# A two-block attention and expert kernel: fp32r maxima, queries prepared inside the attention loop, routing on un-normalised rows, running counts, one delay per group and step

## The chip, the cores and the metric

One core of one Trainium2 chip. The time is device microseconds (us) of one execution, as the median of several runs; fewer is better. The engines are TensorE (PE, with its weight loads as PEld), VectorE (DVE), ScalarE (ACT), GpSimd (POOL) and SyncE (SP), each with an instruction queue of its own that is worked off in order, and the DMA queues.

## The reference

`x` is (2, 512, 128) and `ctx_1024` is (2, 77, 128), fp32. Two blocks run one after the other; each adds an attention and then a layer of experts to `x`:

```
x = x + xattn0(layernorm(x), ctx)        # 16 heads of 8, rotary, a bias, layernorm again inside, gate
x = x + ffn0(layernorm(x))               # top 2 of 8 experts, 128 -> 512 -> 128, silu
x = x + xattn1(layernorm(x), ctx, ctx)   # 16 heads of 8, biases, no gate
x = x + ffn1(layernorm(x))               # top 2 of 8, capacity 321 rows an expert
```

Inside `xattn0` the output is `gate * attended + (1 - gate) * residual` with `gate = sigmoid(attended @ Wgate.T + b_gate)`, where `residual` is the normalised input. The softmax is over 77 keys. The router takes the normalised rows times a (128, 8) matrix, picks two experts by value, and weights their outputs by a softmax over the two.

## The kernel before

The 1,024 tokens are 8 tiles of 128, in 4 **groups** (g = 0 to 3) of 256 tokens. Each block has an attention loop of 16 **units** u (4 per group: four heads at a time), then a tail in which the last groups are finished, then the experts.

**A turn of the loop.** On TensorE (`attention` in the tensor block), turn u does, in this order: `shifted_scores(u)` (L1166, 4 matmuls of 256 columns, in block 0 each with two more of 128 for the bias), `maxima(u+1)` (L1158: the row maxima found by VectorE are turned by two fp32 matmuls of 128 columns against the identity), `scores(u+2)` (L1142), `attend(u-2)` (L1188, 16 small matmuls), and then the steps that are due. VectorE's `attention(u)` (L800) takes the maximum over the scores; ScalarE's (L640) copies the turned maxima into the stack `qst` (L638) and takes the exponential (L654). `scores(u)` waits for the maximum of u-1, `shifted_scores(u)` for the exponential of u-1 and the copied maxima of u.

**The steps.** When a group's four units are attended, ScalarE copies numerator and denominator (L649), and then: `attended` (DVE: reciprocal L813, product L814), `project` (PE), in block 0 `projected` (ACT, then DVE), `gate` (PE) and `tanh` (ACT), then `residual` (DVE: new rows, their statistics), `deviation` (POOL: the reciprocal deviation, L500/L501), `hidden` (DVE: normalised rows, L796/L850), `copies` (ACT), `turn` (PE: transposes of the rows), `turned` (ACT), `logits` (PE), `choose` (DVE: top two), `ranks` (PE: a count of all earlier picks, 1 to 8 matmuls a tile), `slots` (DVE) and `send` (POOL: four indirect DMAs a group). Tables at L71 to L80 give each step on each engine a delay in turns after the group's last unit, one number for all groups, in some cases another for group 3. `due` (L111) goes through the names in the table's order and yields those that fall due. In each engine's queue everything else waits behind a step that waits.

**Queries.** Before a block's loop, the rows are transposed (`tokens`), projected (`queries`), in block 0 rotated (DVE, with the sum on POOL, L566), split into a high and a low part and stacked (`stack`, 8 matmuls of 256 columns, L1310) for groups 0 and 1; groups 2 and 3 follow in the first turns (L83 to L101). In block 0 the rows are normalised twice, with statistics taken of the once normalised rows (L1054 to L1066).

**Warm-ups.** `warm_up` (L1130) are matmuls on zeros: 13 at the start, 12 before block 1, 2 in each turn of block 1's tail, 3 before the experts. They are there for TensorE's clock.

After the tail come the experts (`rows_in`, `up`, `down`), the results go back by indirect DMA, are gathered, and VectorE combines them; block 1 begins with that.

Of the kernel before, what the change touches and what calls it, by code (L numbers as in the profile page):

```python
# [6 lines left out]
B, T, D = 2, 512, 128  # L7
KV = 77
# [35 lines left out]
WARM_START = 13  # L44
WARM_SUM = 12
WARM_TAIL = [0, 2]
# [24 lines left out]
PE_STEPS = [dict(gate3=5, project=4, gate=7, turn=9, logits=10, ranks=11, next_context=8, next_parts=10,  # L71
                 next_keys=11, turn3=7, logits3=9, ranks3=10),
            dict(project=4, turn=7, logits=7, ranks=9)]
DVE_STEPS = [dict(attended=5, projected3=6, residual3=7, hidden3=9, projected=8, residual=9, hidden=10,
                  choose=12, slots=13, next_context=11, next_parts=13, next_keys=14, choose3=11, slots3=12),
             dict(attended=5, residual=7, hidden=8, choose=10, slots=11)]
ACT_STEPS = [dict(projected3=4, tanh3=5, projected=5, tanh=7, copies=8, turned=9),
             dict(copies=9, turned=7)]
POOL_STEPS = [dict(deviation=10, residual=12, send=15),
              dict(deviation=5, residual=7, send=10)]  # L80


PE_QUERIES = [[(-1, "tokens", 0), (-1, "queries", 0), (-1, "keys", 0), (-1, "tokens", 1), (-1, "tokens", 2),  # L83
               (-1, "queries", 1), (-1, "stack", 0), (-1, "queries", 2), (-1, "tokens", 3), (-1, "stack", 1),
               (0, "queries", 3), (1, "stack", 2), (2, "stack", 3)],
              [(-1, "tokens", 0), (-1, "queries", 0), (-1, "tokens", 1), (-1, "tokens", 2), (-1, "queries", 1),
               (-1, "stack", 0), (-1, "tokens", 3), (-1, "queries", 2), (-1, "stack", 1), (0, "queries", 3),
               (1, "stack", 2), (2, "stack", 3)]]
ACT_QUERIES = [[(-1, "tokens", 0), (-1, "keys", 0), (-1, "tokens", 1), (-1, "high", 0), (-1, "tokens", 2),
                (-1, "high", 1), (-1, "stack", 0), (-1, "tokens", 3), (-1, "high", 2), (-1, "stack", 1),  # L90
                (0, "high", 3), (1, "stack", 2), (2, "stack", 3)],
               [(-1, "tokens", 0), (-1, "keys", 0), (-1, "high", 0), (-1, "tokens", 1), (-1, "high", 1),
                (-1, "tokens", 2), (-1, "stack", 0), (-1, "tokens", 3), (-1, "high", 2), (-1, "stack", 1),
                (0, "high", 3), (1, "stack", 2), (2, "stack", 3)]]
DVE_QUERIES = [[(-1, "rotated", 0), (-1, "keys", 0), (-1, "rotated", 1), (-1, "stack", 0), (-1, "rotated", 2),
                (-1, "bias", 0), (-1, "stack", 1), (0, "rotated", 3), (1, "stack", 2), (1, "stack", 3),
                (3, "keys", 1)],
               [(-1, "sum", 0), (-1, "sum", 1), (-1, "norm", 0), (-1, "sum", 2), (-1, "norm", 1),
                (-1, "sum", 3), (-1, "norm", 2), (-1, "norm", 3), (-1, "low", 0), (-1, "low", 1),
                (-1, "stack", 0), (-1, "low", 2), (-1, "stack", 1), (0, "low", 3), (1, "stack", 2),  # L100
                (2, "stack", 3)]]  # L101

WEIGHT_TURNS = [[6, 7, 8, 9], [3, 4, 5, 6]]


def at_turn(queries, turn):

    return [(name, g) for when, name, g in queries if when == turn]


def due(steps, u):  # L111

    for name, delay in steps.items():
        g, rest = divmod(u - delay - (UG - 1), UG)
        if name[-1] == "3":
# [1391 lines left out]
```

## Time and profile before

| | us |
|---|---|
| median of 3 runs | 326.11 |
| lowest and highest of them | 325.69, 334.38 |
| span of the profiled execution | 324.3 |
| TensorE busy | 250.7 |
| VectorE busy | 155.1 |
| GpSimd busy | 137.8 |
| ScalarE busy | 118.2 |

The span is from the first to the last instruction of one profiled execution, and the median includes what lies around it. Busy times overlap between engines.

### The profile page before, as it was taken

How to read it: one execution, taken by the hardware profiler on the slowest of the kernel's cores; microseconds unless marked ns; L12 is line 12 of the kernel's file. 1: busy time of each engine (PE TensorE's matmuls, PEld its weight loads, DVE VectorE, ACT ScalarE, POOL GpSimd, SP SyncE). 2: the span in 40 equal slices, each digit the busy share in tenths (PEclk: the TensorE clock that was granted, in tenths of full speed). 3: DMA queues.
4: the chain of work that ended last, by engine and by line, in shares of the span. 5: the costliest groups of instructions: out<-in, count | busy, mean ns of one | idle time of the engine just before them, and what ended most of it. 6: DMA issues, size and time to landing. Idle time of an engine off the chain costs nothing.

```text
span 324.3 us, 5466 instructions
## 1 busy us (share of the span) xinstructions
PE 250.7 (77%) x2044; PEld 197.2 (61%) x2044; DVE 155.1 (48%) x497; ACT 118.2 (36%) x206; POOL 137.8 (42%) x178
## 2 busy tenths in 40 slices
PE   2767999999975539999942989989987338999800
PEld 2645766667754427999941775545555328999800
DVE  3878425363775364242211964276878303332205
ACT  4033637755321023443500067965540204423200
POOL 5744602630156441355562400641267631456640
PEclk9999999999975558999995799999999959999975
DMA  7999970200011017000013920200010125001015
GB/s 241 269 224 377 219 161 2 65 3 2 0 36 34 33 33 197 16 20 26 23 36 127 361 116 0 66 1 2 0 37 33 33 82 141 15 31 36 26 29 181
DMA packets 26819, 27.02 MB, mean 83 GB/s; under 512 B 3193, under 2 KB 23844, under 8 KB 26534
## 3 DMA queue, kind: packets, MB, share of 16 engines
q1 hardware_dynamic: 23797, 21.58, 24.6%
q0 software_dynamic: 2560, 4.08, 3.9%
q10 hardware_dynamic: 432, 0.98, 0.9%
q8 instruction: 18, 0.29, 0.4%
q14 instruction: 12, 0.09, 0.1%
HBM read 16.76 MB, written 10.79 MB: 85 GB/s over the span
## 4 chain that ended last, share of the span: by engine, by line
PE 49%; issue 20%; DVE 13%; DMA 6%; POOL 5%; ACT 3%; another core or an unknown queue 1%; SPq 1%; POOLq 0%; DVEq 0%; ACTq 0%
PE ps L1201 8%; PE ps L1406 6%; PE ps L1178 6%; PE ps L1395 5%; PE ps L1162 4%; PE ps L1153 4%; PE ps L1133 3%; PE ps L1184 2%; DMA xres<-x 2%; DMA xe<-back 2%; DVE cst L813 2%; DMA sent<-hidk,slotu 1%; DVE attT L814 1%; PE ps L1217 1%
## 5 line engine op out<-in xcount | busy, mean ns | idle before, releaser
L559 POOL DMA_INDIRECT back<-probT,pairu x48 | 46.5, 970 | 37.4 <-DVE probT L992 15.1
L1133 PE MATMUL ps<-blank,ident 128*128 128x256 f32 x90 | 28.6, 479 | 23.6 <-DMA sent<-hidk,slotu 13.0
L1406 PE MATMUL ps<-w,hT 128*128 128x128 f32 (+1 forms) x384 | 45.0, 274 | 0.0
L804 DVE TENSOR_REDUCE peak<-ps 128x8 f32<-128x616 f32 x32 | 25.5, 798 | 40.2 <-PE ps L1153 40.2
L1406 PEld LDWEIGHTS ps<-w,hT 128*128 128x128 f32 (+1 forms) x384 | 44.2, 183 | 0.0
L654 ACT ACTIVATE probT<-ps 77x1024 f32<-77x1024 f32 x32 | 32.7, 1022 | 27.7 <-PE ps L1184 15.5
L518 POOL DMA_INDIRECT sent<-hidk,slotu x32 | 31.9, 997 | 16.4 <-issue 9.8
L1133 PEld LDWEIGHTS ps<-blank,ident 128*128 128x128 f32 x90 | 21.1, 244 | 28.5 <-issue 14.0
L531 POOL TENSOR_TENSOR w1lo<-hT,w1hi 128x1024 fp32r<-128x1024 f32 x8 | 18.9, 2366 | 40.0 <-ACT w1hi L628 40.0
L1178 PE MATMUL ps<-qst,kst 100*78 100x256 f32 x128 | 29.1, 300 | 1.0 <-ACT qst L638 1.0
L500 POOL TENSOR_SCALAR vare<-mv 128x2 f32<-128x2 f32 (+2 forms) x17 | 3.8, 226 | 52.8 <-DVE mv L786 52.3
L696 ACT ACTIVATE hT<-ps,col 128x384 f32<-128x384 f32 x32 | 17.3, 582 | 24.1 <-PE ps L1395 24.1
L696 ACT ACTIVATE hT<-ps 128x321 f32<-128x321 f32 x32 | 13.3, 441 | 33.2 <-PE ps L1395 33.0
L1395 PE MATMUL ps<-xhi,w1hi 128*128 128x384 f32 (+1 forms) x64 | 22.2, 346 | 1.5 <-DVE xlo L981 1.5
L1178 PEld LDWEIGHTS ps<-qst,kst 100*78 100x78 f32 x128 | 16.9, 148 | 8.4 <-issue 5.8
L1162 PE MATMUL ps<-ident,peak 128*4 128x128 f32 x128 | 19.2, 273 | 2.9 <-DVE peak L804 2.9
L1201 PE MATMUL ps<-probT,vpad 77*32 77x256 f32 x256 | 21.0, 391 | 0.0
L1395 PE MATMUL ps<-xhi,w1lo 128*128 128x384 f32 (+1 forms) x64 | 20.8, 325 | 0.0
L1395 PE MATMUL ps<-xlo,w1hi 128*128 128x384 f32 (+1 forms) x64 | 20.8, 325 | 0.0
L1201 PE MATMUL ps<-probT,onepad 77*32 77x256 f32 x256 | 20.2, 379 | 0.0
L992 DVE TENSOR_TENSOR probT<-ps,row 128x128 f32<-128x128 f32 x24 | 5.5, 285 | 26.6 <-PE ps L1406 23.2
L995 DVE COPY probT<-ps 128x128 f32<-128x128 f32 (+1 forms) x24 | 5.5, 284 | 25.4 <-PE ps L1406 21.9
(158 smaller groups left out, 474.1 us busy)
## 6 DMA issues: line engine op xcount, KB each, us to landing
sent<-blank SPq DMA_DIRECT2D x16, 193.5 KB, 8.5
xe<-sent SPq DMA_DIRECT2D x16, 193.5 KB, 4.0
back<-blank SPq DMA_DIRECT2D x16, 128.0 KB, 4.8
hT<-w1b SPq DMA_DIRECT2D x4, 512.0 KB, 6.0
w<-w2b SPq DMA_DIRECT2D x1, 2048.0 KB, 13.5
xe<-back SPq DMA_DIRECT2D x8, 256.0 KB, 3.5
hT<-w1d SPq DMA_DIRECT2D x4, 512.0 KB, 5.5
w<-w2d SPq DMA_DIRECT2D x1, 2048.0 KB, 11.4
```

Of the source, the lines that this page charges most:

```text
L518: pool.indirect_dma_start(sent[m], bass.IndirectOffsetOnAxis(ap=slotu[:, t, k:k + 1], axis=0), hidk[:, t, k, :], None, bounds_check=NSLOT ...
L531: pool.tensor_tensor(w1lo[:, w, :], raw[:, k % RAWS], w1hi[:, w, :].bitcast(F32), ALU.subtract)\
L559: pool.indirect_dma_start(back[m], bass.IndirectOffsetOnAxis(ap=pairu[0:n, e, c:c + 1], axis=0), ye[0:n, e, c, :], None, bounds_check=NPAI ...
L654: act.activation(probT[0:KV, u % RING].rearrange("p (i q) t -> p i (q t)", i=2), ps[0:KV, BK:BK + 2, :], ACT.Exp).then_inc(s_exp[a], 1)
L696: act.activation(hT[:, e % 2, f, 0:CAP[m]], ps[:, 2 + n % 4, 0:CAP[m]], ACT.Silu, bias=bias).then_inc(s_silu[m], 1)
L804: dve.tensor_reduce(peak[:, u % 2], s, AX.X, ALU.max, negate=True).then_inc(s_peak[a], 1)
L1133: pe.matmul(ps[:, bank, 0:GQ], ident[:], blank[:, 0:2, 0:D], start=True, stop=True)
L1162: last = pe.matmul(ps[ST:ST + Q4, BK + u % 2, i * P:(i + 1) * P], peak[:, u % 2, i, :], ident[:], start=True, stop=True)
L1178: last = pe.matmul(ps[0:KP, BK + q // 2, GQ * (q % 2):GQ * (q % 2) + GQ], kst[0:ST + Q4, b, Q4 * j + q, :], qst[0:ST + Q4, j, at:at + GQ], ...
L1201: last = pe.matmul(ps[32 * q:32 * q + 32, bank, 0:GQ], w, probT[0:KV, u % RING, q, :], start=(j == 0), stop=(j == UG - 1))
L1395: last = pe.matmul(ps[:, 2 + n % 4, 0:EVEN[m]], w[:, e, f * P:(f + 1) * P], x[:, e % 2, 0:EVEN[m]], start=(i == 0), stop=(i == len(parts) ...
L1406: last = pe.matmul(ps[0:n, 6 + e % 2, c * P:(c + 1) * P], hT[:, e % 2, f, c * P:c * P + n], w2[:, e, f, :], start=(f == 0), stop=(f == FC ...
```

## The change

- **Maxima** are turned by fp32r matmuls (`peak` and the identity are fp32r), into a PSUM bank of their own.
- **PSUM**: numerator and denominator share one bank (`BND`); `stack` always uses banks 6 and 7; the routing of groups 2 and 3 uses banks 5 and 1.
- **Queries**: only group 0 is made before the loop (and group 1's tokens in block 0); the rest is spread over turns 0 to 9. In block 0 the two normalisations become one (`twice_normed`, from one set of statistics), the rotary sum and the low part go from POOL to DVE, the bias parts from DVE to POOL, the once normalised rows are made in turns 1 and 4. In block 1 the sums of groups 2 and 3 fall in turns 0 and 3. The exponential's table is loaded ahead of the waits.
- **Router**: `turn` transposes the new rows themselves, not the normalised ones; both routers are multiplied by a centring matrix once, in block 0's turn 8, and `choose` scales the logits by the row's reciprocal deviation.
- **Ranks**: a running count of earlier picks; 2 to 3 matmuls a tile.
- **Delays** are given for each group and step; `due` goes through the groups first, then the names. Sends of a group may fall in two halves.
- **Warm-ups**: 6 at the start, 5 and 3 before block 1, a few in the queries' preparation, none behind the loops.

The core of the diff:

```diff
-WARM_START = 13
-WARM_SUM = 12
-WARM_TAIL = [0, 2]
+WARM_START = 6
+WARM_BACK = 3
+WARM_QUERIES = [dict(tokens=1, queries=0, keys=0, stack=3, scores=2), dict(tokens=0, queries=1, stack=2, scores=1)]
+WARM_SUM = 5
...
-PE_STEPS = [dict(gate3=5, project=4, gate=7, turn=9, logits=10, ranks=11, next_context=8, next_parts=10,
-                 next_keys=11, turn3=7, logits3=9, ranks3=10),
-            dict(project=4, turn=7, logits=7, ranks=9)]
-DVE_STEPS = [dict(attended=5, projected3=6, residual3=7, hidden3=9, projected=8, residual=9, hidden=10,
-                  choose=12, slots=13, next_context=11, next_parts=13, next_keys=14, choose3=11, slots3=12),
-             dict(attended=5, residual=7, hidden=8, choose=10, slots=11)]
-ACT_STEPS = [dict(projected3=4, tanh3=5, projected=5, tanh=7, copies=8, turned=9),
-             dict(copies=9, turned=7)]
-POOL_STEPS = [dict(deviation=10, residual=12, send=15),
-              dict(deviation=5, residual=7, send=10)]
+PE_STEPS = [dict(project=(4, 4, 3.5, 4), gate=(6, 6, 4, 6), turn=(8, 8, 6, 7), logits=(9, 9, 7, 7), ranks=(11, 10, 9, 8),
+                 next_context=(0, 0, 0, 9), next_parts=(0, 0, 0, 10), next_keys=(0, 0, 0, 11)),
+            dict(project=(4, 4, 3.5, 4), turn=(7, 6, 4, 5), logits=(8, 7, 5, 5), ranks=(10, 8, 6, 6))]
+DVE_STEPS = [dict(attended=(5, 5, 5, 5), projected=(7, 7, 6, 7), residual=(9, 9, 7, 9), choose=(12, 11, 10, 10),
+                  hidden=(12, 11, 12, 10), slots=(14, 12, 12, 11),
+                  next_context=(0, 0, 0, 12), next_parts=(0, 0, 0, 13), next_keys=(0, 0, 0, 14)),
+             dict(attended=(5, 5, 5, 5), residual=(7, 7, 6, 7), choose=(11, 10, 7, 8), hidden=(11, 10, 10, 8),
+                  slots=(13, 11, 10, 9))]
+ACT_STEPS = [dict(projected=(5, 5, 4, 4), tanh=(7, 7, 5, 6), turned=(9, 9, 7, 7), copies=(11, 10, 11, 8)),
+             dict(turned=(8, 7, 5, 5), copies=(10, 9, 8, 6))]
+POOL_STEPS = [dict(deviation=(9, 9, 7, 10), send=(14, 12, 13, 12), send_second=(14, 12, 15, 12)),
+              dict(deviation=(7, 7, 6, 10), send=(13, 11, 13, 12), send_second=(13, 11, 15, 12),
+                   residual=(14, 14, 17, 13))]
...
+PE_QUERIES = [[(-1, "tokens", 0), (-1, "queries", 0), (-1, "tokens", 1), (-1, "keys", 0), (-1, "stack", 0),
+               (0, "queries", 1), (1, "tokens", 2), (3, "stack", 1), (4, "queries", 2), (4, "tokens", 3),
+               (6, "stack", 2), (7, "queries", 3), (9, "stack", 3)],
+              [(-1, "tokens", 0), (-1, "queries", 0), (-1, "stack", 0), (0, "tokens", 1), (1, "queries", 1),
+               (3, "stack", 1), (4, "tokens", 2), (5, "queries", 2), (6, "stack", 2), (7, "tokens", 3),
+               (8, "queries", 3), (9, "stack", 3)]]
...
+DVE_QUERIES = [[(-1, "rotated", 0), (-1, "values", 0), (-1, "low", 0), (-1, "keys", 0), (-1, "stack", 0),
+                (0, "norm", 1), (0, "rotated", 1), (1, "hidden", 0), (2, "low", 1), (3, "stack", 1),
+                (4, "rotated", 2), (4, "hidden", 1), (5, "low", 2), (5, "keys", 1), (6, "stack", 2),
+                (7, "rotated", 3), (8, "low", 3), (9, "stack", 3)],
+               [(-1, "sum", 0), (-1, "sum", 1), (-1, "norm", 0), (-1, "norm", 1), (-1, "low", 0), (-1, "stack", 0),
+                (0, "sum", 2), (1, "norm", 2), (2, "low", 1), (3, "stack", 1), (3, "sum", 3), (4, "norm", 3),
+                (5, "low", 2), (6, "stack", 2), (8, "low", 3), (9, "stack", 3)]]
+
+CENTRE_TURN = 8
+WEIGHT_TURNS = [[5, 6, 7, 9], [3, 4, 5, 7]]
...
-    for name, delay in steps.items():
-        g, rest = divmod(u - delay - (UG - 1), UG)
...
+    for g in range(GROUPS):
+        for name, delays in steps.items():
+            if delays[g] and u == UG * g + UG - 1 + delays[g]:
+                yield name, g
...
-        peak = sb("peak", [P, 2, GT, Q4])
+        peak = sb("peak", [P, 2, GT, Q4], F32R)
...
+                dve.wait_ge(s_rstd, group[0] + 1)
+                for t in range(GT * g, GT * g + GT):
+                    lp = ps[:, route_bank(g), t % GT * E:t % GT * E + E]
+                    if m == 0:
+                        last = dve.scalar_tensor_tensor(out=logit[:, t, :], in0=lp, scalar=rstd[:, t:t + 1], in1=gbias[:],
+                                                        op0=ALU.mult, op1=ALU.add)
...
             for u in range(turns(DVE_STEPS[0])):
                 attention(0, u)
+                if u == CENTRE_TURN + AHEAD:
...
-                    last = pe.matmul(ps[ST:ST + Q4, BK + u % 2, i * P:(i + 1) * P], peak[:, u % 2, i, :], ident[:],
-                                     start=True, stop=True)
+                    at = GQ * (u % 2) + i * P
+                    last = pe.matmul(ps[0:Q4, BMX, at:at + P], peak[:, u % 2, i, :], identr[:], start=True, stop=True)
...
             def turn(m, g):
-                pe.wait_ge(s_hid[m], g + 1)
...
+                pe.wait_ge(s_xnew[m], g + 1)
+                if m == 0 and g == 0:
+                    pe.wait_ge(s_rout, 2)
+                if g == 1:
+                    pe.wait_ge(s_slot[m], 1)
...
+                transposed(route_bank(g), lambda k: xres[:, GT * g + k, :], GT).then_inc(s_hTp[m], 1)
...
+                earlier = [(ones, before[:, g, :])] if g >= 1 else []
                 for k in range(GT):
...
+                    last = summed(P + k * E, earlier + [(ones, picked[:, t + i, :]) for i in range(k)]
+                                  + [(tri, picked[:, t + k, :])])
...
                     query_steps(a, u + 2)
+                    steps_due(u - 0.5)
                     if u + 1 < UNITS:
                         maxima(a, u + 1)
```

## Rows read from the trace of the kernel before

**Rows 1.** Windows by stage: from:to, length, busy us of each engine, PEclk, DMA.
```profile
0.00:32.20 32.20, 19.34 (x116) 15.21 (x116) 22.40 (x87) 9.64 (x16) 17.10 (x41) 1.00 1.04 278
32.20:90.70 58.50, 57.85 (x590) 39.57 (x590) 28.57 (x58) 32.50 (x49) 18.11 (x15) 1.00 0.31 64
90.70:120.70 30.00, 16.02 (x116) 12.35 (x112) 17.27 (x83) 5.66 (x12) 16.68 (x19) 0.56 0.11 36
...
194.00:242.50 48.50, 45.58 (x452) 26.21 (x450) 30.48 (x76) 30.29 (x44) 17.09 (x16) 1.00 0.06 18
242.50:264.50 22.00, 9.96 (x74) 7.50 (x70) 10.26 (x50) 3.64 (x8) 15.11 (x17) 0.85 0.10 33
```

**Rows 2.** Timeline, a turn of block 0: start, length, engine, line, operation.
```profile
44.74 0.29 PE L1184 MATMUL ps<-btok,bkey 98*78 98x128 f32 x2
44.87 0.29 PE L1178 MATMUL ps<-qst,kst 100*78 100x256 f32 x1
...
45.75 0.60 PE L1162 MATMUL ps<-ident,peak 128*4 128x128 f32 x4
...
46.28 0.55 PE L1153 MATMUL ps<-kst,qst 96*128 96x312 f32 x2
...
47.95 0.29 PE L1184 MATMUL ps<-btok,bkey 98*78 98x128 f32 x2
```

**Rows 3.** Groups of instructions by line: count, busy us, mean ns, idle before.
```profile
L804 DVE TENSOR_REDUCE peak<-ps 128x8 f32<-128x616 f32 x32 | 25.5, 798 | 40.2 <-PE ps L1153 40.2
...
L813 DVE RECIPROCAL cst<-cst 128x256 f32<-128x256 f32 x8 | 14.0, 1744 | 0.0
```

**Rows 4.** Source line 414 (the last router load) and block 0's first shifted scores.
```profile
L414 SPq DMA_DIRECT2D router<-wr x1: 490/490/490, 4.6 to 4.6; - x1
...
DMA to landing us min/median/max: 8.4/8.4/8.4
...
32.21 0.34 PE L1178 MATMUL ps<-qst,kst 100*78 100x256 f32 x1 [0.34 <-ACT qst L638]
```

**Rows 5.** Timeline, late in block 0, and the last send in the chain.
```profile
73.72 0.36 PE L1178 MATMUL ps<-qst,kst 100*78 100x256 f32 x1
...
84.21 0.43 DVE L814 TENSOR_TENSOR attT<-cst 128x256 f32<-128x256 f32 x1
...
85.17 0.39 ACT L661 ACTIVATE norm<-ps 128x256 f32<-128x256 f32 x1 [1.65 <-PE ps L1227]
...
94.51 0.42 DVE L814 TENSOR_TENSOR attT<-cst 128x256 f32<-128x256 f32 x1
...
118.10 2.45 DMA sent<-hidk,slotu
```

**Rows 6.** Block 1: timeline, and the chain's wait behind the last ranks.
```profile
176.73 8.42 PE L1133 MATMUL ps<-blank,ident 128*128 128x256 f32 x24 [10.63 <-DMA xe<-back]
...
194.05 0.63 PE L1178 MATMUL ps<-qst,kst 100*78 100x256 f32 x4
...
216.24 0.72 PE L1178 MATMUL ps<-qst,kst 100*78 100x256 f32 x4
...
245.55 0.42 DVE L814 TENSOR_TENSOR attT<-cst 128x256 f32<-128x256 f32 x1
...
254.56 2.23 another core or an unknown queue
...
262.31 2.24 DMA sent<-hidk,slotu
```

**Rows 7.** Windows of 2 and 1 us around two idle times of TensorE.
```profile
28.00:30.00 2.00, 0.15 (x2) 0.13 (x3) 1.90 (x5) 0.42 (x2) 0.64 (x1) 1.00 1.10 461
...
94.00:95.00 1.00, 0.01 (x1) 0.01 (x1) 0.96 (x3) 0.00 (x0) 0.38 (x1) 0.52 0.08 29
```

**Rows 8.** Source line 814: shortest, median and longest product of eight, in ns; POOL's low weights.
```profile
L814 DVE TENSOR_TENSOR attT<-cst x8: 424/425/2041, 55.8 to 245.5; 128x256 f32<-128x256 f32 x8
...
L531 POOL TENSOR_TENSOR w1lo<-hT,w1hi 128x1024 fp32r<-128x1024 f32 x8 | 18.9, 2366 | 40.0 <-ACT w1hi L628 40.0
```

## What was predicted before the run

> **What bounds the kernel now.** I read the windows by stage first, then the timeline of each stage, then the chain. Each block has a preparation, an attention loop, a tail, and experts with their sends. In both loops TensorE is busy nearly all the time (57.85 of 58.5 us, 45.58 of 48.5) and VectorE half or more of it; in the tails TensorE is busy half the time, and in block 0's, which has no warm-ups, at a clock of 0.56 against 0.85 in block 1's [rows 1]. A turn of block 0 takes 3.21 us (47.95 less 44.74). The maxima hold TensorE for 0.53 of them (45.75 to 46.28); the scores and attending take what is left to the next turn, 1.5 [rows 2]. On VectorE a turn needs one maximum, 0.80 [rows 3], so it has some 2 us a turn for steps. In the tails the order is a single file: attended, project, residual, turn, logits, choose, ranks, slots, sends. The experts and what lies behind them aren't touched. I count in four marks for each block: the first shifted scores, those of a later turn (12 in block 0, 8 in block 1), the last `attT`, and the landing of the last send.
>
> **Fp32r maxima.** The nearest row for the new form is the pair of bias matmuls, also fp32r with 128 columns: the next matmul starts 0.13 after the pair (44.74 to 44.87) [rows 2]. So 0.53 becomes 0.13, less 0.40 a turn, if TensorE is what the turn waits for: 12 turns to the second mark give 4.8 in block 0, 8 give 3.2 in block 1. Bounds: 0, where another engine sets the turn, and 0.40 in all 32 turns, 12.8.
>
> **Block 0, preparation.** The rows of one normalisation are ready at about 10.8 instead of 15.7 (one set of statistics and one pass less). But TensorE also waits for all row loads before the loop, and the last, issued at 4.6, lands 8.4 later, at 13.0 [rows 4]; that is late next, and the gain is cut by 2.2. From 13.0 I follow the queues with the lengths that these steps have in the trace: tokens and their copy 1.5, queries 1.1, rotation and sum on VectorE 1.3, `values` 0.9 (it lies ahead of `low`), low part, krep and stack_keys to 19.7, the stacks to 20.5, scores at 20.6, their maximum till 22.0. Behind it VectorE makes batch 1's rows (1.1), and TensorE has `tokens 2`, which waits for them, ahead of the first shifted scores: 23.6 against 32.2 [rows 4]. **-8.6**. Bounds: -6 (POOL's bias parts, which now stand between, late, or the clock half for a time) and -11 (no wait for batch 1).
>
> **Block 0, turns 0 to 11.** Before: 32.21 to 73.72, 41.5 [rows 4, 5]. Taken off: 4.8. Added to TensorE inside the loop: three stacks, two projections and one set of tokens, 5.3, less the stack that was there, 1.0; group 0's `turn` and the centring, 0.7. The first four turns wait for VectorE, which has a maximum and 1.1 to 2.4 of other work in each (rows of batch 1, two rotations, `hid`, `keys`), and `stack 3` and `project` of group 1 wait too: its `attended` now stands behind `residual` of group 0 on VectorE, since `due` goes by groups. Together 2.3. Sum -4.8 + 5.0 + 2.3: **+2.5** (bounds 0 and +5).
>
> **Block 0, turn 12 to the last `attT`.** Before: 73.72 to 94.93, 21.2. Here the order costs. In the trace the product of group 2 is done at 84.6, before group 1's tanh even starts (85.17) [rows 5]. Now both `residual` of group 1 (4+3+9) and `attended` of group 2 (8+3+5) fall in turn 16 of VectorE, and the residual comes first. It waits for the tanh, which on ScalarE stands behind the exponential of turn 14, the maxima of 15 and now `copies` of group 0 (0.4). In time from turn 12's start: tanh done 11.4, residual and statistics 13.1, reciprocal 1.74 [rows 3] and product 15.4. TensorE has `project` of group 2 at 14.5, ahead of three attends, ready from 11.9: a wait of 3.5. Queued behind it: attend 13, turn, gate of group 2 (1.5, which now also precedes attend 14), attend 14, logits, attend 15, done at 21.8 instead of 16.9. ScalarE's numerator copy waits for nothing worse, but VectorE has choose (1.5), hidden (0.6), residual (1.7) and slots (0.9) ahead of the last `attended`: 27.8. **+6.6**. Bounds: 0 (the tanh gets through early) and +9.
>
> **Block 0, tail.** Before: 94.93 to 120.55, 25.6 [rows 5]. Now groups 1 and 2 are further on. After `attT`: project and yT 2.3, gate 2.9 at the low clock, tanh and new rows 1.4, turn, copy and logits 2.2, choose 1.6, ranks 0.5, slots 0.9, sends 5.4, landing 2.45, with the waits between them 20.2. Gone from the path are statistics, deviation and normalised rows ahead of `turn` (some 2.3), group 2's choose ahead of group 3's, and most of the count: the last ranks and the wait behind them stand for some 2.2 to 2.6 (the chain's wait of 2.23 in block 1 [rows 6]). **-5.4** (bounds -2 and -9). Block 0 together -4.9.
>
> **Block 1.** *Preparation*: TensorE is in warm-ups until 185.15 (176.73 and 8.42 [rows 6]) while the first rows are ready at 181.2. With 5 for 12 they are over by then, 3.7 to the good. `norm 1` no longer waits for group 2's sum, only one stack precedes the scores, and the table load (1.3) lies ahead of the rows: first shifted scores at 188.3 for 194.05: **-5.8** (bounds -3.5 and -8). *Turns 0 to 7*: before 22.2 (194.05 to 216.24 [rows 6]). -3.2 for the maxima, +3.7 for the queries' work inside, +3.0 of waits: `sum` (2.0) ahead of maxima 1 and 4 on VectorE, `tokens 2` and `stack 2` behind them. **+3.5**. *Turn 8 to the last `attT`*: before 29.7. -3.2; group 1's `turn` in turn 13 waits for `slots` of group 0, which VectorE has in turn 16, behind choose, hidden, residual and a maximum, 3.0; group 2's turn, logits and choose are now ahead of the last reciprocal, 1.7. **+1.5**. *Tail*: before 18.6 (245.97 to 264.55). No statistics ahead of `turn`, fewer counts, against a deviation that on POOL stands behind two of group 2's sends (2.5), and transposes and logits at the lower clock (0.44 and 0.61 in this tail, 0.66 and 1.02 in block 0's): **-1.9**. Block 1 together -2.7.
>
> **What lies beside.** The running count (two small additions) and the router's scaling (0.2 each) are behind work that no one waits for; the shared bank `BND` holds as many matmuls as the two before. The keys for block 1 now follow the last slots on VectorE; they end some 2 us before the first expert rows are there. That cover gone, each further us is one.
>
> **The sum.** -4.9 - 2.7 = -7.6 on the span of 324.3: 316.7. The median lies 1.8 above that span: 318.5.
>
> **Two rules.** The trace shows the clock at 0.52 in the window 94.0 to 95.0, in which TensorE was busy for 0.01, but at 1.00 in 28.0 to 30.0, busy for 0.15 [rows 7]. The Trainium skill, "TensorE: Matmul & The Clock Gate", section "What's actually happening", says that the throttled state is the default and that activity lifts it; by that rule the waits of 3.5 and 3.0 above, and the tail without warm-ups, all fall to the low clock, and the rows agree only in part. What it would do here is the third rival.
> The trace has the product of `attended` at 0.42 mostly and once at 2.04, where POOL's low weights (2.37) ran [rows 8]. The Trainium skill, "SBUF — State Buffer", section "SBUF: two separate sides", says that VectorE's operations with two SBUF inputs and GpSimd's share a port pair that one holds for its whole instruction. The rotary sum and the low part become such operations on VectorE, beside POOL's bias parts; by that rule they lose up to one POOL instruction each, the trace agrees for the product, and the range has it.
>
> **Rivals.** *(a) The forecast*, 312 to 325: 0.48.
> *(b) The waits aren't met*: VectorE keeps up, the product of group 2 and the slots of block 1 come in time. Then the +6.6 is -1.6, the +2.3 and the +3.0 (twice) go: about -24 in all, 302; half of it 310. For it speaks that VectorE is busy in only half of the loop [rows 1]; against it, that these waits come from the order in the queues, not from load. 300 to 312: 0.25.
> *(c) Nothing measurable*: the gains in the preparation are given back whole in the loops, by waits at their upper bounds (+5, +9) and by locks. 323 to 332: 0.17.
> *(d) Slower: the clock.* In each wait inside the loops TensorE falls to its low level. A turn then costs 2.8 more than its 2.8. Three turns in all at the low level eat the gain of 7.6; from a little over five (14.5 by 2.8) it is slower by 2%: 333. Against it speaks that the clock stayed at 1.00 through the idle 28.0 to 30.0 [rows 7] and through both loops [rows 1]. 0.10.
>
> **Range and chances.** (a), (b) without its best part, and the near part of (c) give 303 to 328. A change under about 2% (6.5 us) can't be told from none here, so faster means under 319.6: all of (b) and two thirds of (a), 0.57; within 2%: a third of (a) and most of (c), 0.32; slower: (d) and the end of (c), 0.11.
>
> **What would show it.** Maxima: the next matmul 0.13 behind them, and a plain turn of 2.8 in block 0, 2.3 in block 1. Preparation: first shifted scores near 23.6, and 5.8 nearer to the gathered rows in block 1. Order: TensorE idle before group 2's project in block 0 and before group 1's turn in block 1, 3 us each. Clock: 1.00 in both loops. The forecast is wrong if those idle times are missing (then b), if the clock line dips inside a loop (then d), or if a plain turn keeps its 3.2.

## The result, and the profile after

| | before | changed |
|---|---|---|
| median of 4 runs, us | 326.2 | 339.98 |
| lowest and highest | 325.69, 334.38 | 336.5, 347.23 |
| span of the profiled execution | 324.3 | 335.3 |

The ratio is 1.033, 95% interval 1.030 to 1.036: slower by 3.3%, where 318.5 was forecast. (The ratio compares the undisturbed executions, of the changed kernel those of 336.5 and 337.05, and so do all ratios below; `e5_stall` and `e11_lock` have no ratio on record, and their two undisturbed times are given.)

Windows of the changed kernel by the stages of [rows 1]: length, busy us of PE, PEld, DVE, ACT, POOL, the granted clock, DMA.

```profile
0.00:23.80 23.80, 15.39 (x86) 11.99 (x87) 14.98 (x53) 6.90 (x10) 12.94 (x38) 1.00 1.03 250
23.80:88.00 64.20, 54.93 (x536) 40.76 (x536) 39.81 (x82) 33.42 (x52) 18.14 (x13) 0.92 0.40 105
88.00:125.40 37.40, 24.58 (x143) 15.63 (x141) 16.85 (x91) 4.97 (x12) 18.02 (x20) 0.50 0.09 29
...
197.00:244.00 47.00, 41.01 (x348) 27.30 (x349) 27.09 (x67) 27.31 (x42) 13.01 (x11) 0.79 0.04 12
244.00:275.50 31.50, 15.73 (x110) 8.90 (x108) 15.37 (x80) 6.91 (x13) 19.86 (x24) 0.50 0.10 33
```

Both loops of the kernel before had TensorE at 1.00 and, in block 0, busy for 57.85 of 58.5 [rows 1]. Now the first loop is at 0.92 with 9 us idle, the second at 0.79, and the last attends have slipped into the stretches at 0.50. Windows of 3 us tell where the clock falls:

```profile
48.00:51.00 3.00, 0.60 (x3) 0.60 (x4) 3.00 (x2) 0.94 (x1) 2.07 (x1) 0.86 0.45 149
51.00:54.00 3.00, 3.00 (x19) 2.19 (x22) 2.13 (x3) 1.30 (x2) 0.00 (x0) 0.50 0.02 5
54.00:57.00 3.00, 3.00 (x19) 1.96 (x12) 0.70 (x2) 0.58 (x2) 2.35 (x1) 0.50 0.00 0
57.00:60.00 3.00, 2.97 (x36) 2.13 (x36) 0.94 (x3) 1.56 (x3) 0.00 (x0) 1.00 0.00 0
84.00:87.00 3.00, 0.07 (x1) 0.07 (x1) 2.89 (x7) 0.71 (x1) 0.94 (x2) 0.55 0.00 0
87.00:90.00 3.00, 3.00 (x18) 2.13 (x22) 1.03 (x6) 0.47 (x1) 1.25 (x1) 0.50 0.01 3
...
194.00:197.00 3.00, 1.66 (x11) 0.91 (x9) 2.51 (x8) 1.91 (x4) 0.93 (x2) 0.99 0.03 14
197.00:200.00 3.00, 2.37 (x11) 2.29 (x12) 0.57 (x2) 1.06 (x2) 0.00 (x0) 0.50 0.00 0
209.00:212.00 3.00, 3.00 (x22) 2.19 (x14) 0.52 (x2) 1.24 (x3) 2.36 (x1) 0.50 0.00 0
```

In each place TensorE idles first (0.60 busy of 3, 0.07 of 3, 1.66 of 3), and what follows is done at 0.50, although TensorE is busy for 3.00 of 3 again (2.37 in the window 197 to 200). In the window 51 to 54 it gets through 19 matmul records, in 57 to 60 through 36. The timeline of the changed kernel names the waits (in brackets: idle time and what ended it):

```profile
44.22 2.38 POOL L557 TENSOR_TENSOR w1lo<-hT,w1hi 128x1024 fp32r<-128x1024 f32 x1 [4.07 <-ACT w1hi L665]
44.48 2.41 DVE L1029 TENSOR_TENSOR q<-q,ropeb 128x256 f32<-128x256 f32 x1
47.73 2.34 POOL L557 TENSOR_TENSOR w1lo<-hT,w1hi 128x1024 fp32r<-128x1024 f32 x1 [1.12 <-ACT w1hi L665]
47.99 2.36 DVE L1038 TENSOR_TENSOR qlo<-q,qhi 128x256 fp32r<-128x256 f32 x1 [0.39 <-ACT qhi L760]
50.40 0.53 PE L1409 MATMUL ps<-qhi,sel 128*96 128x256 f32 x1 [2.52 <-DVE qlo L1038]
...
83.09 0.43 DVE L878 SCALAR_TENSOR_TENSOR hidb<-norm,hidb 128x256 f32<-128x256 f32 x1 [2.94 <-ACT norm L701]
83.55 0.42 DVE L880 SCALAR_TENSOR_TENSOR xres<-hidb,base 128x256 f32<-128x256 f32 x1
...
84.70 1.72 DVE L858 RECIPROCAL hid<-hid 128x256 f32<-128x256 f32 x1
86.45 0.42 DVE L859 TENSOR_TENSOR attT<-hid 128x256 f32<-128x256 f32 x1
86.93 1.22 PE L1291 MATMUL ps<-attT,sqw 128*128 128x256 f32 x2 [3.27 <-DVE attT L859]
...
242.60 0.66 PE L1215 MATMUL ps<-identr,xres 128*128 128x128 f32 x2 [2.90 <-DVE slotu L950]
```

There are three kinds. (1) VectorE's rotary sum and low part of group 3 begin 0.26 behind GpSimd's subtraction and end 0.28 behind its end. They take 2.41 and 2.36, where the rotary sum takes 0.43 and the low part 0.41 to 0.92 in the other groups: the last stack is 2.5 late. (2) The order: group 1's residual and statistics ahead of group 2's reciprocal, so `project` of group 2 waits 3.27 (the prediction's 3.5), and group 1's `turn` in block 1 waits 2.90 for group 0's slots (the prediction's 3.0). (3) In block 1's first turns there are four short waits in a row, 0.67, 1.14, 0.72 and 0.62. Behind each kind, TensorE's work takes about twice as long.

In turns without extra steps or waits the change does what it says. The maxima are followed at 0.12 (22.58 to 22.70), and units 3 to 4 are 2.77 apart, against 3.20 in [rows 2].

### The profile page after: what moved, and what is told of

It is laid out like the page before. It is cut to its first block, busy times and chain, and to the rows that moved or that the text cites. A ratio compares the mean times of both kernels' runs of the same rounds, so it can differ in the third digit from the quotient of the medians.

```text
span 335.3 us, 5249 instructions
## 1 busy us (share of the span) xinstructions
PE 250.8 (75%) x1911; PEld 197.2 (59%) x1911; DVE 159.4 (48%) x506; ACT 117.1 (35%) x206; POOL 134.7 (40%) x175
## 4 chain that ended last, share of the span: by engine, by line
PE 53%; DVE 16%; issue 12%; POOL 8%; DMA 5%; ACT 4%; POOLq 1%; DVEq 0%; SPq 0%; ACTq 0%
PE ps L1514 9%; PE ps L1275 8%; PE ps L1503 8%; PE ps L1256 5%; PE ps L1210 4%; POOL back L584 4%; PE ps L1409 3%; PE ps L1232 2%; POOL sent L544 2%; PE ps L1262 2%; DMA xe<-back 2%; DMA back<-probT,pairu 2%; PE ps L1215 2%; DVE hid L858 2%; PE ps L1304 1%
## 5 line engine op out<-in xcount | busy, mean ns | idle before, releaser
L849 DVE TENSOR_REDUCE peak<-ps 128x8 fp32r<-128x616 f32 x32 | 25.4, 793 | 37.0 <-PE ps L1232 37.0
L1210 PE MATMUL ps<-blank,identr 128*128 128x256 f32 x60 | 22.3, 529 | 17.8 <-DMA sent<-hidk,slotu 9.1
L1256 PE MATMUL ps<-qst,kst 100*78 100x256 f32 x128 | 31.6, 324 | 1.0 <-ACT qst L675 0.5
L526 POOL TENSOR_SCALAR vare<-mv 128x2 f32<-128x2 f32 (+1 forms) x13 | 2.9, 226 | 65.7 <-DVE mv L831 65.7
L1210 PEld LDWEIGHTS ps<-blank,identr 128*128 128x128 f32 x60 | 15.1, 269 | 21.9 <-issue 9.9
L1275 PE MATMUL ps<-probT,vpad 77*32 77x256 f32 x256 | 25.1, 470 | 0.0
L1256 PEld LDWEIGHTS ps<-qst,kst 100*78 100x78 f32 x128 | 18.7, 163 | 9.6 <-ACT qst L675 6.3
L1275 PE MATMUL ps<-probT,onepad 77*32 77x256 f32 x256 | 24.3, 459 | 0.0
L1232 PE MATMUL ps<-kst,qst 96*128 96x312 f32 x64 | 17.7, 360 | 0.5 <-ACT qst L768 0.4
## 6 DMA issues: line engine op xcount, KB each, us to landing
w<-w2d SPq DMA_DIRECT2D x1, 2048.0 KB, 11.1
```

What stands on the lines that cost most here:

```text
L849: dve.tensor_reduce(peak[:, u % 2], s, AX.X, ALU.max, negate=True).then_inc(s_peak[a], 1)
L1210: pe.matmul(ps[:, bank, 0:tiles * D], ident, blank[:, 0:tiles, 0:D], start=True, stop=True)
L1232: last = pe.matmul(ps[:, BS + i, 0:Q4 * KP], qst[0:ST, j, at + i * P:at + (i + 1) * P], kst[0:ST, b, Q4 * j:Q4 * j + Q4, :].rearrange("p q ...
L1256: last = pe.matmul(ps[0:KP, BK + q // 2, GQ * (q % 2):GQ * (q % 2) + GQ], kst[0:ST + Q4, b, Q4 * j + q, :], qst[0:ST + Q4, j, at:at + GQ], ...
L1275: last = pe.matmul(ps[32 * q:32 * q + 32, BND, den * GQ:den * GQ + GQ], w, probT[0:KV, u % RING, q, :], start=(j == 0 and not den), stop=( ...
```

## Experiments

Each run is compared with the kernel before on the same chip; in brackets the 95% interval.

**Fillers in front of the waits** (`e1_fill`).

```diff
+FILL_QUERIES = [{('stack', 3): 4}, {'maxima 0': 1, 'maxima 1': 2, ('stack', 1): 1, ('tokens', 2): 1}]
+FILL_STEPS = [{('project', 2): 6}, {('turn', 1): 5}]
+            def fill(n, half):
+                for _ in range(n):
+                    pe.matmul(ps[64:P, BMX, GQ * half:GQ * half + GQ], ident[:, 64:P], blank[:, 0:2, 0:D],
+                              start=True, stop=True)
```

> The changed kernel with short matmuls on zeros put in front of seven of TensorE's waits inside the two loops (4 before the last stack and 6 before group 2's project in block 0; 1, 2, 1 and 1 in the first turns and 5 before group 1's turn in block 1), about as long as the idle times there. No wait is shortened and no work is taken away. Theory A (the clock): the idle times bring TensorE to its low level, and the turns behind them run at 0.50 of the clock. Then both loops stay at 1.00, the stretches 50.4 to 57.1, 86.9 to 99.2, 197 to 214.7 and 242.6 to 256.4 shrink by about 3, 5, 6 and 5, and the kernel takes 318 to 325, less than the kernel before. Theory B (only the waits and the work that was moved): the clock is a by-product, the kernel takes 335 to 342 as the changed one, or more by what the fillers add.

Measured: 325.52, ratio 0.997 (0.990 to 1.004): 3.6% or 12 us less than the changed kernel, by adding work only, and at the upper end of what theory A gave. Windows with the filled waits in it:

```profile
48.00:51.00 3.00, 2.60 (x17) 1.60 (x15) 2.63 (x2) 1.79 (x3) 2.35 (x1) 1.00 0.62 175
84.00:87.00 3.00, 2.46 (x19) 1.57 (x21) 2.25 (x8) 0.24 (x1) 0.55 (x1) 1.00 0.00 0
197.00:200.00 3.00, 3.00 (x32) 2.05 (x31) 2.44 (x9) 1.49 (x4) 0.93 (x2) 1.00 0.03 5
239.00:242.00 3.00, 1.51 (x23) 0.73 (x23) 2.82 (x12) 0.78 (x2) 0.88 (x3) 0.97 0.07 22
```

From 33 on the clock stays up until the last attends (before that, 27 to 30 is at 0.50, see the last section), and what TensorE waits for isn't there sooner (the product of group 2 ends at 85.5, 15.0 behind unit 12, and in the changed kernel too it is 15.0). Theory A holds and gives the size: the low clock behind the waits costs 12 us (13.9 in the loops of the two traces), all of the 11 that the changed kernel lost. Without it the change is worth nothing measurable.

**A wait in the kernel before** (`e5_stall`), with nothing of the change:

```diff
+AGAIN = [{8: 6}, {6: 2}]
+                    for n in range(AGAIN[a].get(u, 0)):
+                        n = 6 * a + n
+                        dve.tensor_reduce(wover[:, n, :].rearrange("p (i q) -> p i q", i=GT), s, AX.X, ALU.max, negate=True)
```

> The kernel before, with nothing of the change: VectorE repeats the maximum of unit 8 of block 0 six more times (into a tile that nothing reads) and that of unit 6 of block 1 twice more. VectorE has about 1.3 to spare in a turn, so TensorE should wait some 3.3 once in block 0 and under 1 once in block 1. Theory A (clock): behind the wait in block 0 TensorE runs at 0.50 for several us; the kernel takes the 4 of the waits and at least 3 more, 333 or more. Theory B (only waits): 330 to 331, with the clock at 1.00 in both loops. If the short wait in block 1 alone brings the clock down too, the length of a wait isn't what decides.

Measured: 334.53 and 335.13, the second with the trace, span 333.4 (the kernel before had 325.9 on that chip); the median of all four executions is 345.6.

```profile
58.03 0.49 PE L1166 MATMUL ps<-ident,peak 128*4 128x128 f32 x3 [2.94 <-DVE peak L808]
```

```profile
54.00:57.00 3.00, 1.09 (x12) 0.95 (x11) 3.00 (x5) 1.43 (x2) 2.35 (x1) 1.00 0.02 5
57.00:60.00 3.00, 1.97 (x14) 0.99 (x18) 2.97 (x4) 1.31 (x2) 0.00 (x0) 0.80 0.60 168
60.00:63.00 3.00, 3.00 (x19) 1.93 (x12) 0.80 (x2) 0.10 (x1) 2.35 (x1) 0.50 0.02 7
63.00:66.00 3.00, 3.00 (x18) 2.41 (x17) 0.00 (x0) 0.93 (x1) 0.00 (x0) 0.57 0.00 0
```

One wait of 2.94 brings the clock down, and the kernel takes some 9 us more (theory A: 333 or more). Units 7 to 12 take 25.5 instead of 19.6: 2.9 of wait and 3.0 behind it. The last send of block 0 is 4.8 late. Another 4, not shown to come from the wait, lie in the two experts' stretches, which took 58.6 and 61.6 here and 56.2 and 59.8 in the trace of before. The short wait in block 1 was 0.67 and left the clock at 1.00.

**GpSimd's subtraction moved** (`e3_weights`), `-WEIGHT_TURNS = [[5, 6, 7, 9]` to `+WEIGHT_TURNS = [[4, 8, 9, 10]`.

> The changed kernel with the casts of the expert weights of block 0 in turns 4, 8, 9 and 10 instead of 5, 6, 7 and 9, so that GpSimd's subtraction of 1024 columns (2.37) doesn't run while VectorE has the rotary sum and the low part of group 3. Theory of the port: both VectorE operations go from 2.4 to about 0.42, the wait of 2.5 before the last stack goes. With theory A (clock) the stretch at 0.50 from 51 to 57 goes too: shifted scores of unit 12 start 6 to 8 sooner than 71.9. With theory B they start 2.5 to 4 sooner. Rival: the VectorE operations are slow for another reason (their operands), and stay at 2.4.

Measured: 340.44, ratio 1.042 (1.037 to 1.048). The rotary sum went to 0.43 in all four groups, the wait before the last stack is gone, and unit 8 started at 52.35 instead of 57.12. But the last subtraction now met the residual, whose first operation waits for the tanh at the same time:

```profile
63.08 2.36 POOL L557 TENSOR_TENSOR w1lo<-hT,w1hi 128x1024 fp32r<-128x1024 f32 x1 [1.78 <-ACT w1hi L665]
63.31 2.41 DVE L878 SCALAR_TENSOR_TENSOR hidb<-norm,hidb 128x256 f32<-128x256 f32 x1 [1.53 <-ACT norm L701]
```

```profile
66.00:69.00 3.00, 0.44 (x2) 0.20 (x2) 2.90 (x8) 0.00 (x0) 0.96 (x2) 0.79 0.00 0
69.00:72.00 3.00, 2.87 (x13) 2.69 (x14) 0.79 (x2) 0.00 (x0) 0.00 (x0) 0.50 0.00 0
...
87.00:90.00 3.00, 3.00 (x29) 1.96 (x18) 1.49 (x6) 1.33 (x4) 0.00 (x0) 0.50 0.00 0
```

The wait came back 16 us later, as 1.53 and 2.46 up to 66.2 and 69.1, and the clock stayed at 0.50 from there to the end of the loop. The theory of the shared port holds for a third operation, which again ends 0.28 behind the subtraction; the rival, that the operations are slow by their operands, is out. An operation with one input in PSUM keeps its length beside the same subtraction (which ran from 56.17 to 58.53):

```profile
56.55 0.42 DVE L868 TENSOR_TENSOR hidb<-ps,hidb 128x256 f32<-128x256 f32 x1 [1.54 <-issue]
```

The gain was lost to the same two effects. That unit 12 would start 6 to 8 sooner was a miss: it started at 70.9, 1 sooner.

**`attended` first** (`e2_order`), in `due`:

```diff
+    return sorted(found, key=lambda step: step[0] != "attended")
```

> The changed kernel, where of the steps due in one turn an `attended` comes first (so group 2's reciprocal and product no longer stand behind group 1's residual on VectorE in turn 16 of block 0). Theory A (clock): the wait of 3.3 before group 2's project goes, and with it the low clock behind it: the last attT of block 0 lands 7 to 9 nearer, at 95 to 97 instead of 104.2, and the kernel is 6 to 9 us faster than the changed one, some 330. Theory B (waits only): it is 3 faster, 335 to 337, with the clock still low from 84 on. If the wait only moves to the next step, nothing changes.

Measured: 340.46, ratio 1.020 (1.010 to 1.030). The traced execution took 346.7, so only the order and the waits are read from it; the two that the ratio goes by took 330.95 and 335.08. The wait before group 2's project is gone and from unit 15's shifted scores to the last `attT` it is 14.0 instead of 21.8. In block 1 the same rule puts slots behind a reciprocal, and the wait before group 1's `turn` grows from 2.90 to 5.05. The ratio is 1.3% or some 4 us better than the changed kernel's, between B's 3 and A's 6 to 9, and the intervals touch. In the trace the clock was low from 51 on already. So this run doesn't tell A from B.

**fp32 maxima again**, in the changed kernel (`e4_fp32`) and with the fillers (`e8_fill_fp32`): `peak` as plain fp32, `ident` for `identr`.

> The changed kernel with the maxima turned by fp32 matmuls again, everything else of the change kept. If the turn is TensorE's: 0.40 more in each of some 25 turns that wait for nothing, 8 to 10 us slower than the changed kernel. If other engines or the waits set the turns: 0 to 4 slower. Theory A adds that more TensorE work in a turn could hold the clock up; then it could even be even with the changed kernel.

> The kernel with the fillers inside the loops, with the maxima turned by fp32 matmuls as before the change. With the clock held, the price of this form can be read alone. If TensorE sets the turns: 0.40 more in each of some 25 turns, 333 to 336. If other engines set them: 326 to 329.

Measured: 1.039 (1.031 to 1.047) against the changed kernel's 1.033, no difference that these runs resolve. With the fillers 1.023 (1.014 to 1.032) against 0.997: 2.6%, 8.4 us. Its stages are longer by 3.2 and 0.6 in block 0's loop and 2.4 and 2.0 in block 1's, 8.2 in all, and units 3 to 4 are 3.20 apart again. The saving of 0.40 a plain turn was real; in the changed kernel it doesn't show. Why fp32 cost so little there (more TensorE work between the waits, or shorter waits) isn't settled. The mean granted clock of the executions of `e4_fp32` that the ratio goes by, 0.83 to 0.85 for the changed kernel's 0.81, points to the first.

**Fillers in the tails** (`e7_tail`): `+WARM_BEFORE = [dict(project=7, gate=4, turn=5, ranks=12), dict(project=12, turn=6, ranks=12)]`. And the kernel before without its own (`e10_no_tail`): `WARM_TAIL = [0, 0]`.

> The kernel with the fillers inside the loops, and with matmuls on zeros also before four or three of group 3's steps in the tails (7, 4, 5 and 12 matmuls of 128 columns in block 0, 12, 6 and 12 in block 1). Theory A for the tail: the clock of 0.50 is what the tails' TensorE steps pay (project, gate, turn and logits of group 3 take 2.1, 2.9, 0.7 and 1.0 there, and half of that at 1.00), so each tail is 2 to 3 shorter: 320 to 322. Rival: the zeros keep TensorE busy at its low level when the step is due, and each tail is 0 to 3 longer: 325 to 331.

> The kernel before with the one edit that takes the warm-ups from block 1's tail. If they held the clock for steps on the path (project, turn and logits of the last group): 1 to 2.5 slower. If the tail is set by VectorE, ScalarE, GpSimd and the sends: no difference, within 1.

Measured: `e7_tail` 0.998 (0.994 to 1.003), no gain on 0.997. The clock was up in it, at 1.00 from 102 to 111 where the run without had 0.50, and still the tails took 21.4 and 15.9 as without. In block 0 the rival is what the traces show: TensorE's `project` and `gate` are on the path there, the gate took 1.7 instead of 2.9, but `project` started 1.25 behind its product instead of 0.06, because zeros were still being worked off at 0.50 before it. The gate ended 6.1 behind the product instead of 6.2. In block 1 TensorE is off the path: group 3's deviation waits on GpSimd for two sends of group 2 in both runs, and starts 5.0 and 5.2 behind the product. What the tails would take at full clock with no zeros in the way was not measured. `e10_no_tail` 1.006 (1.002 to 1.011), 2 us; its traced tail is 17.9 against 18.6, so the 2 us aren't found there, and the traced execution, 324.4, was the fastest of its ten.

**Waits taken away instead of filled** (`e6_all`, `e9_steps`, `e12_no_fill`, `e11_lock`). `e9_steps`, cut to its core (parts of the table lines, with comments added):

```diff
-WEIGHT_TURNS = [[5, 6, 7, 9]
+WEIGHT_TURNS = [[4, 8, 9, 11]
+    return sorted(found, key=lambda step: step[0] != "attended")
-turn=(7, 6, 4, 5), logits=(8, 7, 5, 5)            # TensorE, block 1
+turn=(7, 7, 4, 5), logits=(8, 8, 5, 5)
-residual=(7, 7, 6, 7), hidden=(11, 10, 10, 8), slots=(13, 11, 10, 9)   # VectorE, block 1
+residual=(7, 8, 6, 7), hidden=(13, 10, 10, 8), slots=(12, 11, 10, 9)
-hidden=(12, 11, 12, 10)                           # VectorE, block 0
+hidden=(12, 13, 12, 10)
+FILL_QUERIES = [{}, {'maxima 0': 1, 'maxima 1': 2, ('stack', 1): 1, ('tokens', 2): 1}]
+FILL_STEPS = [{('turn', 2): 1}, {}]
```

`e6_all` has the same casts, `attended` first in block 0 alone, the first of the other moves, much the same fillers in the loops, and the tails' fillers; `e12_no_fill` is `e9_steps` without a filler; `e11_lock` is `e9_steps` with the casts in turns 5, 6, 7 and 9.

> The changed kernel with its waits taken away where the traces show them, rather than filled: casts of the expert weights in turns 4, 8, 9 and 11 (no GpSimd subtraction beside a VectorE operation with two SBUF inputs), `attended` first in block 0, group 1's `turn` and logits of block 1 a turn later and group 0's slots a turn sooner. Fillers only in the first turns of block 1 (1, 2, 1, 1), 2 before group 2's turn, and in the tails. If the waits and the clock behind them are the whole loss, both loops stay at 1.00, the last attT of block 0 lands at 90 to 94, and the kernel takes 312 to 319. If new waits take the place of those removed, or the tails' zeros are in the way: 320 to 330.

> The changed kernel with the steps moved where the traces of the earlier runs show a wait, and no zeros in the tails: expert weights of block 0 cast in turns 4, 8, 9 and 11; `attended` first among the steps of a turn; in block 0 `hidden` and `copies` of group 1 behind the last `attended`; in block 1 group 1's turn and logits one turn later, its residual one turn later, group 0's slots one turn sooner and its `hidden` and `copies` two turns later. Fillers only in the first turns of block 1 and one before group 2's turn of block 0. If the waits and the clock behind them were the loss: both loops at 1.00 to their last attends, the last send of block 0 lands near 106, and the kernel takes 308 to 314. If moved steps make new waits: 317 to 325.

> The same step tables with no filler anywhere in the loops. Theory A (clock): what is left of waits in the first turns of block 1 (1.1 and 0.7 between 194 and 198 of the changed kernel, when TensorE is busy for about 0.6 of the time) is enough to bring TensorE to its low level there, and it stays low for over 10 us: 5 to 8 slower than with the fillers. Theory B (waits only): no slower than with them, or 1 to 2 faster.

> The same step tables and fillers, with the expert weights of block 0 cast in turns 5, 6, 7 and 9 again, as the changed kernel has them. This puts GpSimd's subtraction back beside VectorE's rotary sum and low part of group 3. The port alone: those two take 2.4 each again instead of 0.42, TensorE waits 2.5 before the last stack, and the kernel loses 2.5 to 4. With theory A it loses 3 to 5 more by the low clock behind the wait: 6 to 9 in all.

Measured:

| run | median | ratio | span |
|---|---|---|---|
| `e6_all` | 320.15 | 0.985 (0.979 to 0.991) | 317.2 |
| `e9_steps` | 318.28 | 0.975 (0.966 to 0.985) | 316.0 |
| `e12_no_fill` | 320.89 | 0.980 (0.968 to 0.993) | 318.4 |
| `e11_lock` | 326.85 and 328.68 (traced); all four: 333.1 | | 326.2 |

`e11_lock` differs from `e9_steps` by the two collisions alone. Its window 48 to 51 and the one behind it:

```profile
48.00:51.00 3.00, 0.48 (x5) 0.34 (x4) 2.64 (x2) 1.31 (x3) 2.34 (x1) 1.00 0.56 172
51.00:54.00 3.00, 3.00 (x28) 1.93 (x27) 2.97 (x4) 1.81 (x3) 0.33 (x1) 0.64 0.02 5
54.00:57.00 3.00, 3.00 (x18) 2.28 (x11) 0.18 (x1) 0.07 (x1) 2.02 (x1) 0.50 0.00 0
```

and in `e9_steps`:

```profile
48.00:51.00 3.00, 3.00 (x33) 2.18 (x33) 1.87 (x4) 0.94 (x2) 0.00 (x0) 1.00 0.00 0
```

Unit 8 starts 33.8 behind unit 0 in the one and 27.6 in the other, and the last send of block 0 lands at 117.5 and 110.1, 7.4 later. Not all of that is the collisions': 1.3 arose between units 1 and 4, where the code is the same and the clock of `e11_lock` was at 0.66 and 0.77 from 27 to 33. From unit 4 to unit 12 it is 34.0 against 28.2, so the two collisions cost 5.9: 2.5 of wait, the rest behind it, at the lower end of what A said. The span is 10.2 longer, but 2.9 of it lie in block 0's experts, which took 58.6 and 55.7.

`e12_no_fill` is a miss for A. Block 1's first turns have the same four waits as in the changed kernel (0.67, 1.13, 0.72 and 0.62), and behind them the clock was low for about one window:

```profile
185.00:188.00 3.00, 2.17 (x12) 1.81 (x12) 1.59 (x4) 1.66 (x3) 0.00 (x0) 0.80 0.00 0
188.00:191.00 3.00, 2.38 (x12) 1.74 (x11) 1.58 (x4) 1.56 (x3) 0.00 (x0) 0.63 0.00 0
```

The stage lost 1.1, not 5 to 8. The same waits cost the changed kernel a stretch of 17 us at 0.50. How long TensorE stays at its low level isn't told by the wait.

`e9_steps` beats both kernels, though it missed the 308 to 314 that it was meant to reach. The last send of block 0 landed at 110.1 for 106, and behind unit 15 of block 1 it has waits of 1.99 and 1.89, the clock falls at 222, and the last `attT` is 18.6 away.

**The last turns** (`e13_block1`, `e14_both`): group 1's ranks and slots and group 2's project, turn, logits and choose behind attends 14 and 15 or behind the last `attended`.

> The tables with the steps moved, and further in the last turns: in block 1 group 2's project behind attend 13 with one filler before it, group 2's turn, logits and choose one or two turns later and group 1's ranks and slots two turns later, so that nothing that waits for VectorE stands before attends 14 and 15; in block 0 group 1's slots behind the last `attended`. If the low clock from 222 on comes from the waits of 1.99 and 1.89 there: the clock stays at 1.00 until about 228, the last attT of block 1 lands 12 to 14 behind the shifted scores of unit 15 instead of 18.6, and the kernel takes 311 to 314. If the moved steps come back as a longer tail: 315 to 320.

> As the run before, and in block 0 the residual, turn, logits and choose of group 2 behind the last `attended` too. The last reciprocal of block 0 starts 1.6 sooner. If the order in front of the last `attended` sets the end of block 0's tail: 1 to 2 faster than without it. If group 2's steps are then late for GpSimd's sends, of which there are eight behind one another, the last send lands no sooner: equal or 1 to 3 slower.

Measured: `e13_block1` 0.975 (0.969 to 0.981), the same as `e9_steps`; `e14_both` 1.002 (0.998 to 1.006). In `e13_block1` the last `attT` of block 1 is 13.0 behind unit 15, 5.6 sooner as expected, and the tail is 21.3 instead of 15.7, 5.6 longer. Its chain of the tail (start, length, engine, tile, line):

```profile
239.57 0.97 POOL sent L545
240.85 0.97 POOL sent L545
242.12 0.98 POOL sent L545
243.42 0.49 issue
244.13 0.99 POOL sent L545
245.43 0.97 POOL sent L545
246.75 0.73 POOL rstd L528
249.28 0.52 DVE hidk L842 x2
...
255.17 2.24 DMA sent<-hidk,slotu
```

The late slots of group 1 put GpSimd's sends in front of group 3's deviation, which `choose` waits for. What is taken from the loop by moving steps back is paid in the tail.

`e14_both` is a miss: it is nearly 9 us slower than `e13_block1`, where 1 to 3 at most were expected. Its last reciprocal of block 0 starts at 85.00 for 85.84, but as far behind unit 15 (10.4) in both, so the 1.6 didn't come. TensorE then waited 6.64 before group 3's gate, since VectorE had group 2's steps ahead of it, and of these `choose` waited 6.59 for a deviation that on GpSimd stood behind sends. The last send of block 0 starts 7.0 later.

## Why the prediction was wrong, step by step

The terms, in us against the trace of before, from the same four marks a block (the experts' stretch of block 0 ends with VectorE's first operation on the gathered rows, and block 1's preparation begins there):

| term | predicted | changed | `e1_fill` | `e9_steps` |
|---|---|---|---|---|
| block 0 preparation | -8.6 | -8.4 | -8.3 | -9.4 |
| turns 0 to 11 | +2.5 | +6.6 | +5.1 | -0.5 |
| turn 12 to last `attT` | +6.6 | +11.1 | +6.5 | +2.7 |
| tail | -5.4 | -4.5 | -4.4 | -3.3 |
| block 1 preparation | -5.8 | -5.9 | -5.9 | -5.9 |
| turns 0 to 7 | +3.5 | +9.2 | +3.8 | +3.8 |
| turn 8 to last `attT` | +1.5 | +5.3 | +2.9 | +5.7 |
| tail | -1.9 | -3.1 | -2.7 | -2.9 |
| experts, both | 0 | +0.6 | +4.3 | +1.3 |
| sum | -7.6 | +10.9 | +1.3 | -8.4 |

- **Preparation.** Right, to 0.2 in both blocks: first shifted scores at 23.80 for 23.6, held up by batch 1's rows as the prediction had it. That it is so close is partly luck, since runs whose code is the same up to there start them at 22.6 to 24.1.
- **The order.** Right: the two waits, 3.27 and 2.90, are where the prediction put them and as long.
- **Maxima.** Right in size for a plain turn, 0.43, but the sum took 0.40 in every turn of three stages, 4.8, 3.2 and 3.2. `e8_fill_fp32` against `e1_fill` has 3.2, 2.4 and 2.0 there, and 0.6 in the fourth: 8.2 for 11.2 (9.0 if the clock's dip of `e1_fill` at 27, 0.8, is taken out). One row was also misread: from 46.28 to 47.95 it is 1.67, not 1.5 [rows 2]; the sum doesn't use it.
- **The clock, rival (d).** This is the step that failed. The waits were in the sum at their own length, and what follows them at full clock; the rival that prices it had 0.10. Measured, the loops' four terms are 18.1 above the forecast; with the clock held they are 4.2 above it. The evidence against (d) was the clock at 1.00 through both loops, which had no such waits, and one row, 1.00 through 28.0 to 30.0 at 0.15 busy [rows 7]. That row shows that an idle stretch can pass without a fall, not that it will. The row beside it, 0.52 at 94.0, showed the other case, and the forecast itself set two waits of 3 or more inside loops at 1.00. The Trainium skill, "TensorE: Matmul & The Clock Gate", section "What's actually happening", has the low level as the default that activity lifts. The sentence on it in the prediction stood beside the sum and changed no chance. `e1_fill` and `e5_stall` agree with it.
- **The collision.** The prediction named rotary sum and low part as operations that can be locked out, and took GpSimd's bias parts as what they meet. They met the low weights, 2.37, which `WEIGHT_TURNS` puts into the same turns. That is a mis-sized term: nothing in the sum, 3.9 of VectorE and 2.5 of TensorE's wait measured, and with the clock behind it 5.9 (`e11_lock`). The 2.5 and the smaller gain from the maxima more than cover the 4.2 that is left with the clock held. The Trainium skill, "SBUF — State Buffer", section "SBUF: two separate sides", has it that one of the two holds the port pair for its whole instruction. The rows agree: 2.41, 2.36 and 2.41 beside subtractions of 2.34 to 2.38, each ending 0.28 behind the subtraction, and 0.42 for L868 of `e3_weights`, which has one input in PSUM.
- **Tails.** Right within 1.2. The prediction charged them for the low clock. `e7_tail` bears that out only in part: in block 0 the gate did pay for it, but zeros in front of the steps cost what the clock gave back; block 1's tail is set by GpSimd's sends.
- **Gains that stayed away.** With the waits taken out (`e9_steps`) the sum is -8.4, about what was forecast for the changed kernel. That agreement is luck: the terms are others than the forecast's.

## What to carry to other kernels

A wait that a change puts inside a loop that runs at full clock isn't priced at its length: the work behind it can run at half speed, here for 3 to over 20 us. Fill such waits or take their causes away before the change is judged. When an elementwise operation is moved to VectorE, look up what GpSimd runs in the same turn as well as what VectorE has to spare. And where steps are moved later in a loop, follow the sends to the end: 5.6 us won in front of the last `attended` came back as 5.6 in the tail.

## What the runs showed of the hardware

- How far the clock falls behind the same waits isn't fixed. In the first turns of block 0 the code of `e1_fill` and of the changed kernel is the same. Windows of the changed kernel:

```profile
24.00:27.00 3.00, 2.13 (x21) 1.73 (x20) 2.93 (x9) 1.83 (x3) 0.21 (x1) 1.00 1.04 375
27.00:30.00 3.00, 2.43 (x22) 2.03 (x20) 1.24 (x2) 1.69 (x4) 2.49 (x2) 1.00 1.04 438
```

and of `e1_fill`:

```profile
24.00:27.00 3.00, 2.12 (x20) 1.73 (x19) 2.93 (x9) 1.74 (x3) 0.13 (x1) 0.96 0.99 317
27.00:30.00 3.00, 3.00 (x19) 3.00 (x18) 1.31 (x2) 1.52 (x3) 2.57 (x2) 0.50 1.13 472
```

With 2.1 busy of 3 in both, the one stays at 1.00 and the other does the next 3 us at 0.50, which costs it 0.8 up to unit 4.

- Once low, the clock can stay low with TensorE busy for nearly all of each window: from 51 to 57 in the changed kernel, from 203 to 212 in the same trace, and from 69 to 90 in `e3_weights`.
- The experts' stretches, whose code no edit touches, took either 55.7 to 56.8 or 58.1 to 58.8 in block 0, and either 59.6 to 59.8 or 61.3 to 61.8 in block 1, over all traces but those of 345 us and more and that of `e14_both`. In the trace of before TensorE is at 1.00 from 126 on, in `e1_fill` from 129 on, though its warm-ups begin 1 sooner. What decides between them isn't shown, so the last term of the table is not put down to an edit.
- Matmuls on zeros hold the clock up: the four filled windows of `e1_fill` are at 1.00, 1.00, 1.00 and 0.97, where the changed kernel fell to 0.50 in or behind each wait.
